# Feed-forward 0 started 17 slots behind cross attention 0 in a two-layer decoder, with the outer products of its taps on GpSimd

## The reference

```python
x = _layernorm(x + _L0_attn_ref(x, ...))      # causal attention, 16 heads, fake-quantised keys and values
x = _layernorm(x + _L0_xattn_ref(x, ctx, ...))  # cross attention to 77 context rows, 16 heads
x = _layernorm(x + _L0_ffn_ref(x, ...))       # ternary w1, depthwise convolution, silu, ternary w2
x = _layernorm(x + _L1_attn_ref(x, ...))      # recurrence over 1024 positions
x = _layernorm(x + _L1_xattn_ref(x, ctx, ...))
x = _layernorm(x + _L1_ffn_ref(x, ...))
```

```python
def _L0_ffn_ref(x, w1, conv_w, conv_b, w2):
    h = bit_linear(x, w1)                       # x in 8 bits by row, w1 in -1, 0, 1; 256 -> 1024
    h = depthwise_conv1d(h.transpose(0, 2, 1), conv_w, conv_b)   # three taps along the tokens
    h = jax.nn.silu(h.transpose(0, 2, 1))
    return bit_linear(h, w2)                    # 1024 -> 256

def step(state, bu_t):                          # _L1_attn_ref, 1024 steps, 4 x 64 states
    state = jnp.tanh(state * Aexp + bu_t)
```

## Time and profile before

| | us |
|---|---|
| median of 3 runs | 2229.32 (2228.78 to 2234.58) |
| the profiled execution, its own time | 2234.12 |
| its span in the profile | 2232.1 |
| mean granted TensorE clock | 0.862 of full |

### The profile page before, as it was taken

How to read it: one execution, slowest core, us unless ns; L and a number is a source line. 1 busy time by engine, 2 the same in 40 slices (tenths; PEclk the granted TensorE clock), 3 DMA queues, 4 the chain that set the end, 5 groups by cost and what they waited for, 6 DMA issues and landing times. The chain is left out here.

```text
span 2232.1 us, 36088 instructions
## 1 busy us (share of the span) xinstructions
PE 1726.7 (77%) x11992; PEld 1068.5 (48%) x11992; DVE 1745.6 (78%) x4446; ACT 1379.1 (62%) x3471; POOL 888.6 (40%) x983
## 2 busy tenths in 40 slices
PE   7789999999977778775567775547499999955665
PEld 4333333333345666664445554435266667723333
DVE  4788888888637888887878888874378878769997
ACT  1116666666733434433078888889999996246665
POOL 2431000000018886655233433310286686534443
PEclk9898999999979988996668887776699999967766
DMA  2101111111021000000000000001000000010000
GB/s 74 49 13 26 30 28 28 31 31 28 13 68 34 13 10 13 13 6 1 1 15 20 1 1 1 1 1 36 24 1 20 1 1 1 1 36 17 17 20 19
DMA packets 42488, 41.29 MB, mean 18 GB/s; under 512 B 16044, under 2 KB 34352, under 8 KB 42304
## 3 DMA queue, kind: packets, MB, share of 16 engines
q1 hardware_dynamic: 42303, 39.00, 6.5%
HBM read 21.79 MB, written 4.19 MB: 12 GB/s over the span
## 5 line engine op out<-in xcount | busy, mean ns | idle before, releaser
L823 ACT ACTIVATE ST<-ST,aexp 128x1 f32<-128x1 f32 x2046 | 583.2, 385 | 2.4 <-PEq L58 2.4
L623 ACT ACTIVATE PT<-PS 128x512 f32<-128x512 f32 x576 | 309.8, 597 | 153.3 <-PE PS L374 122.1
L514 DVE CUSTOM_DVE_ANT_0 junk<-PS,maskw 128x128 bf16<-128x128 f32 (+3 forms) x512 | 226.8, 486 | 27.9 <-PE PS L351 27.8
L351 PE MATMUL PS<-KT,QT 48*128 48x512 bf16 (+3 forms) x768 | 180.3, 337 | 33.1 <-DVE MX L514 17.9
L517 DVE TENSOR_REDUCE MX<-PS 128x1 f32<-128x512 f32 x256 | 164.5, 684 | 30.0 <-PE PS L351 27.1
L395 PE MATMUL PS<-PT,VP 128*32 128x256 f32 (+1 forms) x2560 | 184.2, 370 | 0.0
L95 PE MATMUL PS<-ident,X 128*128 128x128 f32 x256 | 61.6, 328 | 134.9 <-DVE X L142 131.1
L673 POOL TENSOR_SCALAR nm<-MX 128x16 f32<-128x16 f32 x32 | 6.5, 204 | 377.6 <-DVE MX L520 377.6
L1500 DVE SCALAR_TENSOR_TENSOR U<-U,f_cw 128x128 f32<-128x128 f32 x512 | 152.4, 370 | 0.0
L1773 PE MATMUL PS<-Y,l_pT 128*128 128x256 f32 (+1 forms) x640 | 143.7, 379 | 2.7 <-issue 2.7
L1757 PE MATMUL PS<-Q,l_xT 128*128 128x512 f32 (+1 forms) x384 | 143.9, 525 | 1.7 <-DVE l_s L1807 1.7
(11 more groups left out here) (315 smaller groups left out, 4404.6 us busy)
## 6 DMA issues: line engine op xcount, KB each, us to landing
KT<-KS SPq DMA_DIRECT2D x192, 32.0 KB, 2.0
QT<-QS SPq DMA_DIRECT2D x192, 32.0 KB, 2.0
X<-in_x SPq DMA_DIRECT2D x8, 512.0 KB, 3.7
Y<-in_x SPq DMA_DIRECT2D x32, 128.0 KB, 2.0
out<-j_xn SPq DMA_DIRECT2D x32, 128.0 KB, 1.7
QT<-NMT SPq DMA_DIRECT2D x192, 2.0 KB
U<-in_L_ffn_w SPq DMA_DIRECT2D x2, 1024.0 KB, 6.8
...
```

Source lines behind the costliest of these rows:

```text
L351: T.matmul(bank(u % 3)[:, 0:w * P], QT[i % R][rows, qt * P:(qt + 1) * P], KT[i % R][rows, k0 * P:(k0 + w) * P], start=True, stop=True).the ...
L514: V.tensor_tensor_reduce(junk[u % 3][:, 0:w * P], bank(u % 3)[:, 0:w * P], maskw[:, BANK - w * P:], 1.0, NEG, ALU.add, ALU.max, MX[i % 2][ ...
L623: C.activation(PT[n % 4][:, 2 * pr + e, 0:w], bank(3 + u % 3)[:, 0:w], ACT.Exp, scale=0.25).then_inc(e_done, 1)
L823: C.activation(self.ST[:, m, t:t + 1], self.ST[:, m, t - 1:t] if t else self.zero[:, :], ACT.Tanh, bias=self.BU[:, m, t:t + 1], scale=self ...
```

## The change

LAG becomes 17: cross attention alone has slots 0 to 16, both run in 17 to 40, feed-forward alone in 41 to 52. The weights' first slots move from 3, 9 and 5 to 2, 7 and 4. Three value units a slot are run instead of two; on ACT the third copy stands after the second group of states, on PE the third product after the products Bu and Du. `act_states` is called with 10 while cross attention runs, and `keys` issues 60 steps. PE's transposes of the quantised h (hqtr) move into the cross part of the slot, between the two halves of the probability transposes. The two outer taps become two products on POOL, of all eight groups at once (`g` = h * w left, and in place on `h` with w right), and two `tensor_add` on DVE; the second addition stands later in DVE's slot, behind the copy of yT, and the first ahead of the row maximum.

```diff
--- before.py
+++ after.py
@@ -1050,7 +1050,7 @@
             sp()
             pe()
             dve()
-            act_more(90)
+            act_more(60)
             st.end()
             pre.close()
 
@@ -1210,7 +1210,7 @@
 
 
         ctx, st = ExitStack(), Stage(nc, "cross0")
-        LAST, LAG = NT + 8, 32
+        LAST, LAG = NT + 8, 17
         WIDE, HW = LAST + 1 - LAG, P + 2
         in_Y1, in_Y2, in_U = places(Y1), places(Y2), places(U)
         x = PairedCross(ctx, in_Y1)
@@ -1238,14 +1238,14 @@
         d_o, d_aT, d_mm, d_y, d_xn = st.sems("d_o d_aT d_mm d_y d_xn")
         e_xq, e_ds, e_tr, e_bc, e_xqT, e_rsb, e_zero = st.sems("e_xq e_ds e_tr e_bc e_xqT e_rsb e_zero")
         nC, nD, qE = Norm(st, ctx, "nC", D), Norm(st, ctx, "nD", D), Quant(st, ctx, "qE")
-        conv_in, conv_ready, f_mm, f_h, f_cm, f_cC, f_cL, f_cR, f_silu = st.sems(
-            "conv_in conv_ready mm h cm cC cL cR silu")
+        conv_in, conv_ready, f_mm, f_h, f_cm, f_cC, f_gL, f_hR, f_cL, f_cR, f_silu = st.sems(
+            "conv_in conv_ready mm h cm cC gL hR cL cR silu")
...
         qF, nF = Quant(st, ctx, "qF"), Norm(st, ctx, "nF", D)
-        R.host(st, 5, places(in_hq), places(in_y))
-        w1.host(st, ctx, 3, raw1, rounded1)
-        w2.host(st, ctx, 9, raw2, rounded2, clear=(R.turned, 4))
+        R.host(st, 4, places(in_hq), places(in_y))
+        w1.host(st, ctx, 2, raw1, rounded1)
+        w2.host(st, ctx, 7, raw2, rounded2, clear=(R.turned, 4))
         wide.host(st, places(Y2), ((d_xn, NT), (e_rsb, NT)))
 
         def by_head(a):
@@ -1369,6 +1369,7 @@
             w1.pe_free(j)
             w2.pe_free(j)
             R.pe_free(j)
+            pe_turn_levels(j - LAG)
             if on(f):
                 if f == 0:
                     T.wait_ge(x.w_in, 48)
@@ -1386,22 +1387,25 @@
                 last.then_inc(d_q, 1)
             x.pe(j)
 
-        def pe_ffn(j):
-
-            a, c, d, other = j, j - 3, j - 4, j + LAG
+        def pe_turn_levels(j):
+            d, other = j - 4, j + LAG
             if on(d):
                 T.wait_ge(f_hq, d + 1)
                 if d >= 1:
                     T.wait_ge(f_hqT, d)
                 T.wait_ge(c_y, min(other, NT))
                 transposes(hq[d % 2], bank(6).bitcast(BF16), KH).then_inc(f_hqtr, 1)
+
+        def pe_ffn(j):
+
+            a, c, d, other = j, j - 3, j - 4, j + LAG
             if on(c):
                 T.wait_ge(f_silu, c + 1)
                 if c >= 1:
                     T.wait_ge(qF.scaled_done, c)
                 T.wait_ge(d_pT1, min(other - 4, NT))
                 transposes(g[c % 2][:, :, :].rearrange("p k n -> p (k n)"), bank(4, 2), KH).then_inc(f_gtr, 1)
-            wide.pe(2 * (j - WIDE))
+            wide.pe(3 * (j - WIDE))
             if on(d):
                 T.wait_ge(f_hqT, d + 1)
                 T.wait_ge(d_qT, min(other - 2, NT))
@@ -1423,7 +1427,7 @@
                         last = T.matmul(PS[:, at:at + HW], w1.wT[:, k, q * P:(q + 1) * P],
                                         XQ[:, k, a % B, (a // B) * P:(a // B) * P + HW], start=k == 0, stop=k == KD - 1)
                 last.then_inc(f_mm, 1)
-            wide.pe(2 * (j - WIDE) + 1)
+            wide.pe(3 * (j - WIDE) + 1)
             if on(d):
                 T.wait_ge(f_xn, d + 1)
                 transposes(X[:, d, :], bank(3), KD).then_inc(f_xtr, 1)
@@ -1434,11 +1438,14 @@
                 for k in range(KD):
                     last = T.matmul(bank(3)[:, 0:D], yT[d % 2][:, k * P:(k + 1) * P], R.DwT[:, k, :], start=k == 0, stop=k == KD - 1)
                 last.then_inc(f_bmm, 1)
+            wide.pe(3 * (j - WIDE) + 2)
 
         def pe():
             for j in range(LAG + NT + 4):
                 if j <= LAST:
                     pe_cross(j)
+                else:
+                    pe_turn_levels(j - LAG)
                 if j >= LAG:
                     pe_ffn(j - LAG)
 
@@ -1495,12 +1502,6 @@
             w2.dve(j)
             R.dve(j)
 
-        def tap(i, k, src, dst):
-            for q in range(KH):
-                last = V.scalar_tensor_tensor(dst[i % 2][:, q, :], h[i % 3][:, q, k:k + P], cw[:, q, k:k + 1],
-                                              src[i % 2][:, q, :], ALU.mult, ALU.add)
-            return last
-
         def dve_ffn(j):
             a, b, c, d = j, j - 2, j - 3, j - 4
             if on(d):
@@ -1508,16 +1509,13 @@
                 if d >= 2:
                     V.wait_ge(f_mm2, d - 1)
                 V.tensor_copy(hqT[d % 2][:, :], bank(6).bitcast(BF16)).then_inc(f_hqT, 1)
+            if on(b):
+                V.wait_ge(f_cC, b + 1)
+                V.wait_ge(f_gL, b + 1)
+                V.tensor_add(g[b % 2][:, :, :], g[b % 2][:, :, :], c0[b % 2][:, :, :]).then_inc(f_cL, 1)
             if on(c):
                 V.wait_ge(f_gtr, c + 1)
                 qF.dve_max(c, bank(4, 2))
-            if on(b):
-                V.wait_ge(f_cC, b + 1)
-                if b >= 2:
-                    V.wait_ge(f_gtr, b - 1)
-                else:
-                    V.wait_ge(w2.wb_done, 2)
-                tap(b, 0, c0, g).then_inc(f_cL, 1)
             if on(d):
                 V.wait_ge(f_mm2, d + 1)
                 V.scalar_tensor_tensor(y[d % 2][:, :], bank(3)[:, 0:D], ds[d % 4][:, :], X[:, d, :], ALU.mult, ALU.add).then_inc(f_y, 1)
@@ -1530,9 +1528,6 @@
                 qF.dve_inverse(c)
             if on(d):
                 nF.dve_moments(d)
-            if on(b):
-                V.wait_ge(f_cL, b + 1)
-                tap(b, 2, g, g).then_inc(f_cR, 1)
             if on(d):
                 nF.dve_apply(d, X[:, d, :], y[d % 2][:, :]).then_inc(f_xn, 1)
             if on(c):
@@ -1544,6 +1539,10 @@
             if on(d):
                 V.wait_ge(f_xtr, d + 1)
                 V.tensor_copy(yT[d % 2][:, :], bank(3)[:, 0:D]).then_inc(f_xT, 1)
+            if on(b):
+                V.wait_ge(f_cL, b + 1)
+                V.wait_ge(f_hR, b + 1)
+                V.tensor_add(g[b % 2][:, :, :], g[b % 2][:, :, :], h[b % 3][:, :, 2:P + 2]).then_inc(f_cR, 1)
             if on(c):
                 if c >= 2:
                     V.wait_ge(f_hqtr, c - 1)
@@ -1626,15 +1625,16 @@
 
         def act_ffn(j):
             b = j - 2
-            wide.act(2 * (j - WIDE))
+            wide.act(3 * (j - WIDE))
             if j >= 8:
-                R.act_states(13 if j + LAG <= LAST else 9)
+                R.act_states(10 if j + LAG <= LAST else 9)
             if on(b):
                 C.wait_ge(f_cR, b + 1)
                 C.activation(g[b % 2][:, :, :], g[b % 2][:, :, :], ACT.Silu).then_inc(f_silu, 1)
-            wide.act(2 * (j - WIDE) + 1)
+            wide.act(3 * (j - WIDE) + 1)
             if j >= 8:
-                R.act_states(13 if j + LAG <= LAST else 9)
+                R.act_states(10 if j + LAG <= LAST else 9)
+            wide.act(3 * (j - WIDE) + 2)
 
         def act():
             for j in range(LAG + NT + 4):
@@ -1679,8 +1679,17 @@
                 G.tensor_tensor(c0[m % 2][:, :, :], c0[m % 2][:, :, :], cb[:, :].unsqueeze(2).broadcast_to([P, KH, P]), ALU.add).then_inc(f_cC, 1)
             if on(d):
                 nF.pool_rstd(d)
-            wide.pool(2 * (j - WIDE))
-            wide.pool(2 * (j - WIDE) + 1)
+            if on(m):
+                if m >= 2:
+                    G.wait_ge(f_gtr, m - 1)
+                else:
+                    G.wait_ge(w2.wb_done, 2)
+                G.tensor_tensor(g[m % 2][:, :, :], h[m % 3][:, :, 0:P], cw[:, :, 0:1].broadcast_to([P, KH, P]), ALU.mult).then_inc(f_gL, 1)
+                G.wait_ge(f_gL, m + 1)
+                G.tensor_tensor(h[m % 3][:, :, 2:P + 2], h[m % 3][:, :, 2:P + 2], cw[:, :, 2:3].broadcast_to([P, KH, P]), ALU.mult).then_inc(f_hR, 1)
+            wide.pool(3 * (j - WIDE))
+            wide.pool(3 * (j - WIDE) + 1)
+            wide.pool(3 * (j - WIDE) + 2)
 
         def pool():
             x.pool()
```

## The result

The changed kernel takes **2261.33 us** (median of 4 runs, 2258.78 to 2262.66) against 2231.95 (2228.78 to 2236.31) for the kernel before on the same chip: a ratio of 1.0129, 95% interval 1.0116 to 1.0141, so 29 us slower. The forecast was 2252. The profiled execution has a span of 2260.3 us, 28.2 over that of before.

The account below looks back on a forecast made before the run. Full slots were taken as bound by DVE's chain waiting for Pool, ACT's loop just under. Stage from slot 17 +18, slots 0 to 16 +1, cross attention 1 +3.4: +22.4, from 2229.3 to 2252; range 2237 to 2270, chance 0.45.

Parts of the forecast that it names:

- The blocking: After nF's rstd: DVE's apply waits out Pool's first product, 2.0 instead of 0.40; the wait costs 2.15 us a slot.
- not paid: Rival: DVE's apply and second addition take the ports before Pool's products; full slots 23.3, kernel 2212; chance 0.20.
- The chain of a full slot: Slots 21 to 32: DVE waits for Pool's work up to nF's rstd; 24.0 us, taken as 24.4, ACT's loop 23.3.
- The table loads: ACT's exp and silu: two loads a slot, 34 in all, 1.28 each; rival with the longer switch near 2277, chance 0.03.
- The value slots: Slots 41 to 50, three value units: third ACT copy behind tanh delays PE's unit and mm2; 17.1 us against 13.9.
- Busy time rules: Rival: DVE's busy time sets the slots, full slots 19.2, value slots 13.9; 94 us less, 2158; chance 0.08.
- no change: Rival: overlap pays exactly what drain and value slots cost; full slots at 23, kernel near 2235; chance 0.15.
- Clearly slower: Rival: PE falls to 1.2 GHz in full slots, 27 us each; 39 us more, 2291; chance 0.12.
- Slots 0 to 16: Before the overlap: as before, except earlier weight steps put one more Pool rounding among them; +1 us.
- The keys stage: 60 state steps instead of 90 save 17 us of ACT but no time, as DVE's copies wait for PE; still 51.
- The stage from slot 17: Slot 17 to the keys stage: 64 + 12 x 24.4 + 91.5 + 76 + 169 + 24.5 = 718 against 700; +18.
- Cross attention 1: Later stage: fewer steps done before it, so its last tanh ends six steps later; +3.4 us at most, taken whole.

Follow-up runs that it names:

- the pieces: Each of Pool's two tap products issued as four instructions over two of the eight blocks, against the changed kernel: 2220.08 us, ratio 0.9936.
- moving the copy: ACT's third value-unit copy put ahead of the second group of state steps, against the changed kernel: 2247.64 us, ratio 1.0058.
- with the last units behind the slots: Changed kernel with Pool's products in four pieces each and two value units a slot, the units left over made after the last slot: 2206.97 us, ratio 0.9886.
- at the lag of 24: Changed kernel with Pool's products in four pieces each, two value units a slot and LAG 24 instead of 17: 2204.85 us, ratio 0.9879.
- the lag of 32 with the pieces: Kernel before (lag 32, two value units) with tap products on Pool in four pieces each and the additions on DVE: 2184.36 us, ratio 0.979.

## Why the prediction was right

**The blocking** (the step "what Pool's products block") held by its numbers: apply 1.99 for 2.0, the second addition's end t + 4.9 for t + 5.2 (1006.52 less 1001.59), 23.9 a full slot for 24.4. The rival "not paid" needed DVE to start first. It is 0.07 late in 29 of the 32 slots (the last three applies have no product beside them and take 0.41), near the 0.06 of the earlier trace rows. The forecast and its rival without blocking lay 40 us apart, and short products gave 41; that this is the same number is luck in part. The rival took 2.15 off each of the slots 37 to 50, 30 us, and the pieces gave 17.4 there; it had nothing in slots 17 to 20 and in the keys stage, where they gave 5.0 and 1.9. Nor are pieces the same as no blocking: the apply still takes 0.69. Of the two waits that were priced the second was short, since the addition takes 1.47 for 1.22. The rule of the Trainium skill, "SBUF — State Buffer", section "Who interferes with whom", that I had weighed against the change is borne out in both directions: an addition that is first makes Pool's product take 2.77 for 1.91, and Pool's nC rstd 1.15 for 0.55. It does not hold where Pool's instruction is an rstd: the addition of 1018.75 starts 0.05 behind nD's rstd and takes 1.22, as when it is free.

**The chain of a full slot**, Pool's two operations on 1024 elements up to nF's rstd, is in the timeline: DVE waits 2.54 there. That ACT's loop lies just under it is shown by the kernel in pieces, where it binds at 23.0 (forecast 23.3); without tanh a slot takes 22.5 there.

**The table loads**: 33, where I said 34, at 1.28 each, beginning 0.02 behind the instruction before, with ACT's exp 0.01 behind the load. Of the 2.66 a switch of the Trainium skill, "ScalarE: Activation LUTs", section "What ACT_TABLE_LOAD costs", the load's part (about 1283 ns) is what the trace has, and the drain of 1.38 is not seen here; its rival of 2277 falls.

**The value slots**: 17.2 in slots 42 to 49 for 17.1 (16.0 to 18.9 each), and 166.7 in all ten for 169, by the chain that was named; moving the copy gave back 13.7. The forecast stopped there and did not see that Pool's fills come next.

**Busy time rules** (0.08) and **no change** (0.15) fall: DVE is busy 84% in the full slots at 23.9 a slot. (The rival's 19.2 was too high by its own rows: 321.3 us of 385 at 13.9 a slot are 11.6 of DVE's work, which the additions leave at 9.1 and not 9.7, so 18.6.) **Clearly slower** falls too: a full slot takes under 24.4, at a granted clock of 0.83 in that window (the forecast had leaned on 0.91).

Three terms of the sum were mis-sized: +6.0, +2.1 and -3.4, with 1.0 in the stage from slot 17 (19.0 for 18), turn my 22.4 into 28.1, of the 28.2 between the spans. *Slots 0 to 16*: "+1" was +7.0. I had counted one more Pool rounding and not asked what the earlier weight steps stand ahead of. 0.7 of it was there before the stage began to differ (656.49 for 655.77), 3.3 is w1's sum, 2.3 are w2's last two passes, which lay behind the border before, and the rest, 0.7, I can't place. In three of the other kernels whose slots 0 to 16 are the same code they take 2.0 more (163.6 us for 161.5 from slot 2 on), so a remainder of this size tells nothing. *The keys stage*: "nothing" was +2.1. Its instructions are the same, and PE's granted clock is lower: 0.67 for the 0.71 of the kernel before. In the other kernels with 60 or 90 steps in that stage it goes the same way, 53.0 to 53.2 at 0.67 and 50.4 to 51.5 at 0.70 to 0.73. *The stage from slot 17*: 718.8 for 718 is luck in part, since its terms were off by more and cancel: slots 17 to 20 took 70.7 for 64, 4.7 of it in slot 20 (27.2 for 22.5), where I had not priced the two products on the second addition and the rounding; the full slots took 5.9 less than forecast, 33 to 36 2.6 more, 41 to 50 2.3 less. *Cross attention 1*: "+3.4 at most, taken whole" was 0. The last tanh does end later, 307.0 us after the stage's start for 303.7, and the stage keeps its 406.1. The limit is near: with the last units behind the slots the last tanh ends at 310.4 and the stage takes 409.5, and at the lag of 24, with fewer steps made before, 317.7 and 415.3.

What I did not ask was how good the two parts of the change are each alone. My rows gave the comparison: 11.04 and 13.9 less the gain of the additions, end to end, against 24.4, with the drain slots on top. And 13.9 is the mean of slots with value units and without; a slot without them, which is what a full slot replaces, took 13.7.

What stays open: the last 0.7 us of slots 0 to 16, and why the slots at the lag of 32 with the pieces are long and short by turns (12.4 and 13.1 with value units, 11.8 and 12.3 without); neither was tried.
